# The order of the first and last five batches, and the order of the first loads, in a four-layer cross-attention kernel

## The reference

```
x = L0(x, ctx)          # causal self-attention, layernorm, cross-attention, layernorm, relu MLP, layernorm
x = L1(x, ctx, mask)    # rmsnorm, rotary attention (16 query, 4 key heads of 64), rmsnorm, gated MLP of 1024
x = L2(x, ctx)          # layernorm, cross-attention of 16 heads of 16, residual
x = L3(x, ctx, mask)    # cross-attention, scores scaled by the mask and clipped to 50, residual, layernorm
```

## Time and profile before

| | us |
|---|---|
| three executions | 4020.08, 4020.08, 4019.24 |
| median | 4020.08 |
| profiled execution | 4024.71 |
| its span | 4022.9 |
| TensorE busy / VectorE / ScalarE / GpSimd | 3927.7 / 2945.7 / 2672.9 / 1227.7 |

### The profile page before, as it was taken

The page is one execution under the profiler, slowest core; times in us unless marked ns, Lnnn a source line. Parts: engine busy times, 40 slices in busy tenths (PEclk is TensorE's granted clock), DMA queues, the critical chain, the costliest instruction groups (busy, mean ns, idle before and its releaser), DMA issues.

```text
span 4022.9 us, 115273 instructions
## 1 busy us (share of the span) xinstructions
PE 3927.7 (98%) x44448; PEld 3431.3 (85%) x44448; DVE 2945.7 (73%) x10721; ACT 2672.9 (66%) x8449; POOL 1227.7 (31%) x2247
## 2 busy tenths in 40 slices
PE   6999999999999999999999999999999999999997
PEld 5788888888888888888888888888888888888885
...
DMA packets 66495, 69.61 MB, mean 17 GB/s; under 512 B 7456, under 2 KB 64800, under 8 KB 65056
## 3 DMA queue, kind: packets, MB, share of 16 engines
...
## 4 chain that ended last, share of the span: by engine, by line
PE 89%; DVE 6%; ACT 2%; issue 2%; POOL 1%; DMA 0%; SPq 0%; DVEq 0%; POOLq 0%; ACTq 0%
PE gen_ps L467 54%; PE gen_ps L459 16%; PE gen_ps L589 6%; PE scores_ps L563 5%; PE gen_ps L601 3%; PE scores_ps L549 3%; PE scores_ps L556 2%; PE scores_ps L542 1%; ACT oT L699 1%; DVE wide L887 1%; DVE zn L932 1%; DVE v L992 1%; DVE rdenm L929 1%; DVE plainT L995 1%; DVE res L996 1%
## 5 line engine op out<-in xcount | busy, mean ns | idle before, releaser
L467 PE MATMUL gen_ps<-actT,w_sb 128*128 128x128 f32 x10752 | 1352.7, 279 | 14.1 <-DMA w_sb<-weights_dram 9.3
L467 PEld LDWEIGHTS gen_ps<-actT,w_sb 128*128 128x128 f32 x10752 | 1267.5, 193 | 70.2 <-issue 48.1
L699 ACT ACTIVATE probT<-gen_ps 128x512 f32<-128x512 f32 x1024 | 576.3, 633 | 218.1 <-PE gen_ps L459 214.8
L788 POOL TENSOR_TENSOR rstd<-ve,consts 128x1 f32<-128x1 f32 x448 | 282.7, 631 | 1436.5 <-DVE ve L939 850.9
L733 ACT ACTIVATE prob<-scores_ps,negmax 128x128 f32<-128x128 f32 x2048 | 566.6, 415 | 200.5 <-DVE negmax L977 200.4
L459 PE MATMUL gen_ps<-consts,prob 128*128 128x128 f32 x4096 | 605.6, 279 | 17.4 <-ACT prob L733 7.2
L459 PEld LDWEIGHTS gen_ps<-consts,prob 128*128 128x128 f32 x4096 | 473.0, 142 | 130.2 <-ACT prob L733 59.2
L467 PE MATMUL gen_ps<-w_sb,actT 128*128 128x256 f32 x1792 | 466.6, 383 | 2.9 <-ACT actT L699 2.1
L467 PE MATMUL gen_ps<-w_sb,wide 128*128 128x256 f32 x2056 | 466.7, 380 | 1.3 <-DVE wide L1117 1.0
L849 POOL TENSOR_SCALAR prob<-prob,rden 128x128 f32<-128x128 f32 x1024 | 362.1, 373 | 320.7 <-DVE rden L1050 320.7
L699 ACT ACTIVATE actT<-gen_ps 128x256 f32<-128x256 f32 (+1 forms) x512 | 238.5, 466 | 292.9 <-PE gen_ps L459 292.9
(11 more groups left out here) (116 smaller groups left out, 6013.4 us busy)
## 6 DMA issues: line engine op xcount, KB each, us to landing
...
mask<-mask_dram SPq DMA_DIRECT2D x128, 64.0 KB, 2.1
...
```

Source lines behind the costliest of these rows:

```text
L467: last = nc.tensor.matmul(ps, lhsT(c), rhs(c), start=(c == 0), stop=(c == chunks - 1))
L699: release(nc.scalar.activation(dst, take(act, name, b)[:, 0:width], ACT.Copy), name, b)
L788: nc.gpsimd.tensor_tensor(dst, src, const("expo")[:, 0:width], ALU.pow)\
```

## The change

Three edits of tables and one of a list of loads.

`PERIOD` goes from 69.731652 to 60.594933 and every time in `LIFE` and `ONCE` is new. Sorted without the third edit, the new tables give, on each of the four engines, exactly the list that the old ones give, in all 3970, 3776, 3849 and 1216 steps of PE, ACT, DVE and POOL.

`moment` bends the time of a step in batches 0 to 4 and 59 to 63 by a curve through seven knots. That changes the lists only near the ends: on PE 39 places up to place 257 (of batch 5) and 18 places from place 3763 on, on ACT 15 and 15, on DVE 35 and 20, on POOL 4 and none.

The loads are put in another order, and qk0 and v0 become two loads.

```diff
-PERIOD = 69.731652
+PERIOD = 60.594933
 LIFE = [
-    ("queries", 0, 0, {"PE": 0.000, "DVE": 37.380}),
...
+    ("rows_in", 0, 0, {"DVE": 0.000}),
+    ("queries", 0, 0, {"PE": 5.180, "DVE": 6.864}),
...
+KNOTS = [0.000, 39.742, 79.484, 119.226, 158.968, 198.711, 238.453]
+RAMP = {
+    0: [1.607873, 19.963948, 64.681647, 120.719207, 159.275114, 198.550687, 239.020101],
+    1: [-39.697006, 35.227949, 80.538628, 119.397866, 159.169502, 199.264569, 238.718948],
...
+    B - 1: [-0.100067, 39.846439, 79.971814, 120.214108, 163.515618, 192.643301, 941.532011],
+}
-LOADS = [("first", "qk0", "v0"), ("second", "qk1", "fc2"), ...
+LOADS = [("first", "qk0", "qk0"), ("v0", "v0", "v0"), ("second", "qk1", "fc2"), ...
+def moment(b, time):
+    return PERIOD * b + (float(np.interp(time, KNOTS, RAMP[b])) if b in RAMP else time)
 def order(engine):
-    events = [(PERIOD * b + times[engine], name, a, b, u) for b in range(B) ...
+    events = [(moment(b, times[engine]), name, a, b, u) for b in range(B) ...
...
+                sp.dma_start(actT[:, 0, 2:4, :], xT_d[0]).then_inc(xT_sem(0), 16)
+                fetch(*LOADS[0])
+                sp.dma_start(cols_sb[:, :], cols_d).then_inc(sem("su_cols"), 16)
                 sp.dma_start(consts[:, :], consts_d).then_inc(sem("su_cols"), 16)
-                sp.dma_start(cols_sb[:, :], cols_d).then_inc(sem("su_cols"), 16)
-                fetch_x(0)
-                fetch(*LOADS[0])
+                fetch(*LOADS[1])
+                sp.dma_start(x_in[:, 0, :], x_d[0]).then_inc(x_in_sem(0), 16)
+                fetch_x(1)
+                fetch_ctx(0)
+                fetch(*LOADS[2])
                 sp.dma_start(rows_sb[:, :], rows_d).then_inc(sem("su_rows"), 16)
-                fetch_ctx(0)
-                fetch(*LOADS[1])
-                fetch_x(1)
-                fetch(*LOADS[2])
                 fetch_ctx(1)
```

More of the change, by code:

```diff
@@ new lines @@
+    ("turn", 0, 1, {"PE": 51.908, "ACT": 52.586}),
+    ("turn", 0, 2, {"PE": 53.659, "ACT": 54.337}),
+    ("turn", 0, 3, {"PE": 57.327, "ACT": 57.965}),
+    ("values", 0, 0, {"PE": 62.410, "ACT": 64.398}),
+    ("attended", 0, 0, {"PE": 65.339, "DVE": 66.433, "POOL": 67.623}),
+    ("stats", 0, 0, {"DVE": 68.387, "POOL": 69.302}),
+    ("norm", 0, 0, {"DVE": 69.557, "POOL": 71.279}),
+    ("tr", 1, 0, {"PE": 71.923, "ACT": 72.561}),
+    ("queries", 1, 0, {"PE": 73.214, "DVE": 76.449}),
+    ("keys", 1, 0, {"PE": 74.203, "ACT": 76.162}),
@@ new lines @@
+    ("first_row", 1, 0, {"PE": 77.936, "DVE": 78.578}),
+    ("scores", 1, 0, {"PE": 80.304}),
+    ("soft", 1, 0, {"ACT": 83.847, "DVE": 81.616}),
+    ("soft", 1, 1, {"ACT": 85.795, "DVE": 82.224}),
+    ("soft", 1, 2, {"ACT": 86.791, "DVE": 82.821}),
+    ("ctx_norms", 0, 0, {"DVE": 84.760, "POOL": 110.561}),
+    ("turn", 1, 0, {"PE": 85.163, "ACT": 89.240}),
+    ("soft", 1, 3, {"ACT": 88.244, "DVE": 87.526}),
+    ("turn", 1, 1, {"PE": 90.048, "ACT": 91.107}),
+    ("turn", 1, 2, {"PE": 92.242, "ACT": 93.205}),
@@ new lines @@
+    ("turn", 1, 3, {"PE": 92.678, "ACT": 93.681}),
+    ("values", 1, 0, {"PE": 94.463, "ACT": 95.552}),
+    ("attended", 1, 0, {"PE": 97.392, "DVE": 98.030, "POOL": 99.098}),
+    ("stats", 1, 0, {"DVE": 100.026, "POOL": 100.929}),
+    ("norm", 1, 0, {"DVE": 101.370}),
+    ("x2T", 1, 0, {"PE": 102.719, "ACT": 103.139}),
+    ("h", 1, 0, {"PE": 104.147, "ACT": 105.520}),
+    ("z", 1, 0, {"PE": 106.894, "DVE": 107.975, "POOL": 109.870}),
+    ("norm_x3", 1, 0, {"ACT": 111.147, "DVE": 110.114}),
@@ new lines @@
+    ("turn", 2, 3, {"PE": 143.328, "ACT": 143.966}),
+    ("out2", 2, 0, {"PE": 143.858, "ACT": 145.438}),
+    ("out2", 2, 1, {"PE": 144.745, "ACT": 145.914}),
+    ("o2", 2, 0, {"PE": 147.127, "ACT": 151.305, "DVE": 150.845}),
+    ("mean_square", 3, 0, {"DVE": 151.850, "POOL": 152.084}),
+    ("rms_norm", 3, 0, {"DVE": 152.667}),
+    ("nT", 3, 0, {"PE": 153.708, "ACT": 154.751}),
+    ("gate", 3, 0, {"PE": 156.119, "ACT": 158.079, "DVE": 161.361}),
+    ("up", 3, 0, {"PE": 158.423, "DVE": 162.880}),
@@ new lines @@
+    ("gate", 3, 1, {"PE": 160.181, "ACT": 163.999, "DVE": 164.627}),
+    ("up", 3, 1, {"PE": 165.731, "DVE": 167.756}),
+    ("down", 3, 0, {"PE": 168.804, "DVE": 172.521, "POOL": 173.896}),
+    ("norm_x4", 3, 0, {"DVE": 174.524}),
+    ("tr", 3, 0, {"PE": 175.390, "ACT": 176.028}),
+    ("queries", 3, 0, {"PE": 177.638, "DVE": 179.189}),
+    ("keys", 3, 0, {"PE": 178.953, "ACT": 180.912}),
+    ("scores", 3, 0, {"PE": 182.562}),
+    ("soft", 3, 0, {"ACT": 184.592, "DVE": 183.875}),
+    ("soft", 3, 1, {"ACT": 186.064, "DVE": 184.473}),
@@ new lines @@
+    ("o", 3, 0, {"PE": 200.002, "DVE": 201.233, "POOL": 213.194}),
+    ("tr", 4, 0, {"PE": 203.266, "ACT": 203.889}),
+    ("queries", 4, 0, {"PE": 206.843, "DVE": 207.924}),
+    ("keys", 4, 0, {"PE": 211.674, "ACT": 213.633}),
+    ("scores", 4, 0, {"PE": 214.615}),
+    ("soft", 4, 0, {"ACT": 217.218, "DVE": 215.705}),
+    ("soft", 4, 1, {"ACT": 217.958, "DVE": 216.775}),
+    ("soft", 4, 2, {"ACT": 219.150, "DVE": 217.837}),
+    ("soft", 4, 3, {"ACT": 221.335, "DVE": 220.125}),
+    ("values", 4, 0, {"PE": 224.275, "ACT": 226.234}),
@@ L178 @@
+    ("attended", 4, 0, {"PE": 228.963, "DVE": 232.217}),
+    ("zT", 4, 0, {"PE": 232.985, "ACT": 233.405}),
+    ("o", 4, 0, {"PE": 234.129, "DVE": 235.846, "POOL": 237.209}),
+    ("norm", 4, 0, {"DVE": 237.453}),
 ]
```

65 lines of the change are left out of this document (53 added, 12 removed), and 3 rows, old and new, of the table RAMP.

## The result

The kernel after the change takes 4009.12 us (median of 10 runs, 4006.58 to 4012.47), the kernel before, in the same session, 4019.71 us (10 runs, 4014.11 to 4020.88): a ratio of 0.9974, 95% interval 0.9965 to 0.9984. That is 10.6 us or 0.26% faster (6.4 to 14.1 us by the interval), more than the 8.04 us that the prediction took as what can be told from nothing. The forecast was 6.3 us, rival 1 had 10.5. The profiled execution took 4011.12 us with a span of 4009.3: 13.6 us under the span before. Of these, 3 us are chance: before's profiled run lay 5.0 us above its median, this one 2.0.

What follows compares the result with a forecast made beforehand. The prediction took waits inside the first and last batches to bound the ends and TensorE the middle. Its terms, 4.5 + 0.3 + 1.0 + 0.5 = 6.3 us off 4020.08, gave 4013.8 us, range 4009 to 4018.

Steps and rivals of the forecast that it cites:

- rival 1: Both ends: the clock comes forward to full and loads reach their better bound; 10.5 us, 4009.6 us, chance 0.27.
- The middle: Middle periods: TensorE-bound, 0.23 us idle in 60.85; the new period without the bend was priced at nothing.
- Loads: Start: reordered loads bring the first product from 9.26 to about 7.6 us; gain 1.65 us, bounds 0.8 and 3.3.
- the estimate by strict order alone: Start loads: with no landing lag, the first product starts near 6 us and the forecast is 1.6 us lower.
- Part 2: Start, batch 1's queries, keys and first_row earlier: 0.9 us up to `tr1@0`, 0.8 us before `first_row1@0`.
- a second place where the clock could come forward: Start, `keys0@1`: half-clock products from about 36.5 us could raise the clock for 44 to 52 us; 0 to 2.5, taken 0.3.
- Part 3: Start, batch 2's steps earlier: brings the total lead at `scores1@1` to 4.5 us.
- the two cases weighed: Products from `tr1@1` to `scores1@1`: half clock again, 3.5 us lead; full clock, 1.6 us less work, 5.1 us lead.
- End order: Last batches: steps moved into waits gain 1.0 us in sum, 0.9 of it at `down@63`.
- Last chain's clock: From the last turns to the last store: the clock's fall may come later; 0 to 1.3 us, taken 0.5.
- Hidden anyway (2): Both ends: loads gain 0.8 us and underestimated waits take back queue gains; some 2.5 us, 4017.6 us, chance 0.16 shared.
- half clock to the end (3): Drain: half clock from 3947 us on doubles some 16 us of products; 9.7 us slower, 4029.8 us, chance 0.04.

Runs made afterwards that it cites:

- e5_again: The kernel after the change, unaltered, measured again on another chip: 4014.82 us, ratio 0.9977 to the kernel before.
- e11: The kernel after with extra identity products filling TensorE's waits at both ends: 3996.23 us, ratio 0.9934 to the kernel before.
- e3_start: The kernel before with the new tables bent for batches 0 to 4 alone, old loads and end: 4012.71 us, ratio 0.9983.
- e9_part2: The kernel before with only queries, keys and first_row of attention 0 in batch 1 moved earlier, old loads: 4016.05 us, ratio 0.9982.
- e6_busy_end: The kernel after with extra identity products in TensorE's waits near the end: 4007.01 us, ratio 0.9955 to the kernel before.
- e1: The kernel before with the new order of loads alone, qk0 and v0 split: 4018.0 us, ratio 0.9997.
- e2: The kernel before with only qk0 and v0 made two loads, old order kept: 4017.31 us, a single execution.
- e4: The kernel before with the new tables bent for batches 59 to 63 alone, old loads and start: 4017.36 us, ratio 0.9998.
- e7_busy_start: The kernel after with extra products ahead of the first step and in TensorE's waits at the start: 4006.0 us, ratio 0.9951 to the kernel before.
- e10: The kernel before, order and loads untouched, with extra products filling TensorE's waits at both ends: 4009.24 us, ratio 0.9963.

## Why the prediction was right in its range and off in its size

The time, 4009.12, is within 4009 to 4018 at its very edge; the likeliest number was 4.7 us too high, and a measurable gain, which came, had a chance of only 0.28. To that edge some luck belongs: the same change measured again, e5_again, is 0.23% and not 0.26%. The marks that it gave came early: `tr1@0` at 42.03 for 44.1, `scores1@0` at 53.93 for 55.7, `tr1@1` at 99.00 for 102.5, `scores1@1` at 107.08 for 110.7 to 112.3. Step by step:

- **The middle, nothing.** Right: 60.62 us of products in 60.85 before and after.
- **Loads, 1.65 us.** The step that said "with a lag of 0.6 to 0.9 MB" was mis-sized: 3.0 us in the profile of the result, near the bound of 3.3, lag 0.24 MB; 2.4 in e5_again, lag 0.37. The mark set for being wrong, a first product before 7 us, was hit. The forecast took the large load's lag for the constants, against its own row of 3.3 us for them. The Trainium skill ("DMA: Bandwidth & Descriptors", section "Queues, rings and completion order") has descriptors taken in ring order and completion not first-in first-out; the estimate by strict order alone was near 6 us, and this trace, at 6.25, is nearer to it than to the lag. But e11's, at 8.09, is where the lag of 0.6 to 0.9 MB put it: the landing scatters, and one figure for it was the error.
- **Part 2, 0.9 + 0.8 = 1.7 us.** The queue steps are there in their sum, but small: from the first product to `scores1@0` it is 47.87 to 49.61 us in the four profiles with the old order, 46.97 to 47.68 in the three with the new order and loads, 1.1 us less in the mean. The part up to `tr1@0` alone (36.15 to 37.25 against 35.78 to 36.01) hardly stands out of the scatter. But alone on the old loads they bring 7.2 us by the ratio (3.6 to 10.9). The prediction saw a second place where the clock could come forward and dismissed it with "`betas`, busy 5 us just before, did not raise the clock. I take 0.3". In e3_start and e9_part2 it did rise, before the values of batch 0, with `queries0@1` in the wait that had stood before the turns: `betas` took 2.74 us instead of 5.12. From the first product to `tr1@0` both take 31.71 us. In the kernel after, in e5_again and in e6_busy_end, with the new loads, `betas` again took 5.12, and batch 0's `nT` stands at 118.2, 117.3 and 116.7 us, later than e3_start's 115.78 in spite of a first product 2.3 to 2.9 us earlier. So the two gains don't add there: these five profiles agree, but why the new loads put the rise off wasn't tried.
- **Part 3, to 4.5 at `scores1@1`.** 8.25 measured. Of the excess, 1.35 is the loads and 1.5 to 2.1 is the profile of the kernel before, slow at its start (106.07 us from the first product to `scores1@1`, against 104.0 to 104.6 in e1, e2 and e4). Of the two cases weighed, the full clock came: `queries1@1` and `keys1@1` take 2.05 us instead of 3.38, and from `tr1@1` to `scores1@1` it is 8.08 us instead of 9.70. That is the 1.6 us that the forecast gave to that case before it took the mean of both; the clock gives 1.3 to 1.6 of it (`queries1@1` to `keys1@1`: 1.89 us instead of 3.17, or 3.51 in e1), and what `keys0@2` gives by being gone from there is mostly taken back by DVE, where `first_row0@2` now comes ahead of `first_row1@1`.
- **End order, 1.0 us.** Right and a little small; the medians of e4_end (1.7 us, 0.8 by the ratio) can't tell it from nothing. `scores4@62` to `down@63` fell from 10.54 to 9.34 us, 1.2 for the forecast's 0.9. The wait before `tr3@63` was to be kept at 1.0 us and is 1.84, since TensorE arrives earlier and DVE ends it.
- **Last chain's clock, 0.5.** Half of what went at the end: 2.4 us behind `values3@63`. It is no property of the change but luck: the same list takes 30.0 (e7_busy_start) to 35.1 us (e2_split).
- **Rivals.** Rival 1, with 10.5 us, has the number but not the whole mechanism: the last turns and `keys1@1` did run faster, the stretch from 44 to 52 us mostly not, and with the waits filled in both the change still keeps some 9 us, 2 of them by its loads and an unknown part by a clock that e10 didn't hold as well. Hidden anyway (2) and half clock to the end (3) didn't happen: `down@63` still took 3.72 us.
